# Field-pair projection: from fp32r matmuls on split parts to plain fp32 matmuls of contraction 64 on two partition halves

## The chip, the cores and the metric

The kernel runs on one core of a Trainium2 chip. The metric is the device time of one execution in microseconds (us), the median of several runs. A core has TensorE (matmuls, which write PSUM), VectorE, ScalarE, GpSimd (POOL, which works in SBUF alone in this kernel) and SyncE (SP, which only issues transfers), and 16 DMA engines that all queues share.

## The reference

The input x is 2048 x 32 x 64 (batch, fields, dim), and W holds one 64 x 64 matrix for each of the 496 pairs of fields i < j. The output is 2048 x 496 x 64, 260 MB, all in fp32:

```
xi = x[:, pi, :]
xj = x[:, pj, :]
proj = jnp.einsum('bpd,pod->bpo', xi, W)
return proj * xj
```

So field i is projected by the matrices of all its pairs, and each projection is multiplied element by element by field j.

## The kernel before

**Tiling.** The batch is cut into 16 tiles of 128 rows, which stand on the partitions of the result. For a field i, the pairs (i, i+1) to (i, 31) lie next to each other in the output, so x_i (turned, 64 values of dim on the partitions, 128 rows of the batch as its columns) is the stationary operand and a run of up to 512 columns of weights is the moving one. A run of 1024 columns or less is a *step*: it fills one of three PSUM buffers (`proj`, two banks each). `plan` lists 30 steps in 20 *groups*; a group is what one store writes, and it is staged in one of five SBUF slots (`staged`).

**Precision.** The kernel multiplies in fp32r and makes up for its precision: every value is split into a high part (its top bits, by masking) and a low part (value less high part). The parts of W stand on two partition halves, high over low (`w_t`); the turned parts of x stand once as high over low and once as low over high (`x_t`). Two matmuls that add up in PSUM (L388) give all four products.

**Preparing x.** Per tile, in eight chunks of four fields: VectorE masks (L427), POOL subtracts (L274) and copies the high part once more (L276), TensorE turns eight 128 x 128 blocks through the two PSUM banks `turned` (L373), and ScalarE copies them out into `x_t` (L315). `x_due` says at which steps this is done for the chunk after next.

**Preparing W.** Only in the first tile: 31 chunks of 16 pairs come in, into staging slots and a ring that partly lies in the second x buffer, and go the same way (L441, L282, L373, L322) into `w_t`, spread over the steps of the first tile. The loads of the first 16 chunks are issued by SP at the start, the others by ScalarE as the ring gets free (L329). x of tile 1 is loaded after the last chunk.

**The result.** VectorE multiplies a step in PSUM by x_j and writes the staging slot (L467). For five steps of each tile but the first, ScalarE copies PSUM to the slot instead (L343) and POOL multiplies there (L296). SP issues the store of a group when its last step is done (L234), and after the last group of a tile the load of x for the tile after next, once that x buffer has been split (L240 and L241).

**Order.** Each engine runs its own list in the order in which it is written; semaphores tie them together. TensorE waits for the PSUM buffer to be read (`read_out`), VectorE and ScalarE wait for the slot's store to have landed (`stored`), and SP for the group's results.

Of the kernel before, what the change touches and what calls it, by code (L numbers as in the profile page):

```python
# [5 lines left out]

F32 = mybir.dt.float32
F32R = mybir.dt.float32r
I32 = mybir.dt.int32
# [5 lines left out]
HI_BITS = -4096  # L25
PROJ_BUFS = 3
SLOTS = 5
CHUNK = 4
POOL_FIELDS = (2, 5, 8, 11, 14)
WARM_UP = 16  # L30
W_CHUNK = 16
W_RING = 7
W_SPLIT_SLOTS = (2, 3, 4)

W_LEAD = 1
W_LEAD_FROM = 2
W_GAIN = 4
# [7 lines left out]
def plan(fields, dim):  # L45

    fit = 2 * BANK // dim  # L50
    def whole(*lengths):
        return [(fields - 1 - n, fields - n, n) for n in lengths]
    groups = []
    for i in range(fields - 1 - fit):

        n = fields - 1 - i
        cut = fit if n > fit + fit // 2 else fit // 2
        groups.append([[(i, i + 1, cut)], [(i, i + 1 + cut, n - cut)]])
    groups += [[whole(16), whole(15)], [whole(14), whole(13)], [whole(12), whole(11)],
               [whole(10), whole(9), whole(8)], [whole(7, 6), whole(5, 4), whole(3, 2, 1)]]  # L60
    return groups


def place(step, dim):

    at, places = 0, []
    for _, _, n in step:
# [4 lines left out]
    assert at <= 2 * BANK  # L72
    return places


class Tile:
# [5 lines left out]
    def next(self):  # L82
        return Tile(self.number + 1, 1 - self.parity, self.half + self.parity)


def field_pair_project(nc, x, w, ident, out, fields, dim):
    batch = x.shape[0]
    tiles = batch // P
    groups = plan(fields, dim)
    steps = [step for group in groups for step in group]  # L90
    n_steps, n_groups, chunks = len(steps), len(groups), fields // CHUNK
    pairs = fields * (fields - 1) // 2
    w_chunks = pairs // W_CHUNK
    uses = n_steps // PROJ_BUFS
    slot_uses = n_groups // SLOTS
    assert n_steps % PROJ_BUFS == 0 and n_groups % SLOTS == 0 and chunks % 2 == 0
    assert tiles % 2 == 0 and tiles >= 4 and pairs % W_CHUNK == 0 and 2 * dim == P

    def group_range(group):
        i, j0, _ = group[0][0]  # L100
        k, l0, n = group[-1][-1]
        return pair_index(i, j0, fields), pair_index(k, l0 + n - 1, fields) + 1
    slot_pairs = max(end - first for first, end in map(group_range, groups))

    w_cols = W_CHUNK // 2 * dim
    w_per_slot = slot_pairs * dim // w_cols


    pool_steps = [2 * i + 1 for i in POOL_FIELDS]
    assert all(len(steps[s]) == 1 and steps[s][0][0] == i for s, i in zip(pool_steps, POOL_FIELDS))  # L110


    chunk_starts = {min(s for s, step in enumerate(steps) if step[0][0] >= CHUNK * c): c for c in range(chunks)}
    w_needed = [pair_index(step[-1][0], step[-1][1] + step[-1][2] - 1, fields) // W_CHUNK for step in steps]

    def w_turned_by(s):

        if s < 0:
            return 0
        lead = W_LEAD if s >= W_LEAD_FROM else 0  # L120
        return min(w_needed[s] + w_needed[s] // W_GAIN + lead + 1, w_chunks)

    def w_split_by(s):

        return min(w_turned_by(s) + min(s + 1, 2), w_chunks)

    def x_due(tile, s, ahead):

        due = []
        for start, c in chunk_starts.items():  # L130

            if s == (start + 1 if c == 0 else start):
                if c + ahead < chunks:
                    due.append((tile, c + ahead))
                elif not tile.last:
                    due.append((tile.next(), c + ahead - chunks))
        return due

    def transposes_due(tile, s):

        due = []
        if tile.first:
            if s == 0:
                due.append(("x", tile, 0))
            due += [("w", k) for k in range(w_turned_by(s - 1), w_turned_by(s))]
        return due + [("x", of, c) for of, c in x_due(tile, s, 1)]

    def splits_due(tile, s):

        due = []  # L150
        if tile.first:
            if s == 0:
                due.append(("x", tile, 0))
            due += [("w", k) for k in range(w_split_by(s - 1), w_split_by(s))]
            if s == 0:
                due.append(("x", tile, 1))
        return due + [("x", of, c) for of, c in x_due(tile, s, 2)]

    def each_tile(eng, emit):

        emit(Tile(0, 0, 0))
        with eng.Fori(0, (tiles - 2) // 2) as t:
            emit(Tile(2 * t + 1, 1, t))
            emit(Tile(2 * t + 2, 0, t + 1))
        emit(Tile(tiles - 1, 1, tiles // 2 - 1, last=True))

    with ExitStack() as ctx:
# [3 lines left out]
        def psum(name, cols):  # L171
            return ctx.enter_context(nc.psum_tensor(name, [P, cols], F32))

        def sem(name):
            return ctx.enter_context(nc.semaphore(name))

        w_t = sb("w_t", [P, pairs * dim], F32R)
        x_sb = [sb(f"x_sb{h}", [P, fields * dim]) for h in range(2)]
        x_parts = [sb(f"x_parts{h}", [P, CHUNK, 3, dim]) for h in range(2)]
        x_t = [sb(f"x_t{h}", [P, CHUNK, 2, P], F32R) for h in range(2)]  # L180
        w_parts = [sb(f"w_parts{h}", [P, W_CHUNK // 2, 2, dim]) for h in range(2)]
        ident_sb = sb("ident_sb", [P, P])
        staged = [sb(f"staged{s}", [P, slot_pairs * dim]) for s in range(SLOTS)]


        w_in_x = fields * dim // w_cols
        w_extra = sb("w_extra", [P, (W_RING - w_in_x) * w_cols])
        w_early = [staged[slot][:, n * w_cols:(n + 1) * w_cols]
                   for slot in W_SPLIT_SLOTS for n in range(w_per_slot)]
        w_ring = [x_sb[1][:, n * w_cols:(n + 1) * w_cols] for n in range(w_in_x)]  # L190
        w_ring += [w_extra[:, n * w_cols:(n + 1) * w_cols] for n in range(W_RING - w_in_x)]

        def w_in(k):
            return w_early[k] if k < len(w_early) else w_ring[(k - len(w_early)) % W_RING]
        proj = [psum(f"proj{b}", 2 * BANK) for b in range(PROJ_BUFS)]
        turned = [psum(f"turned{k}", BANK) for k in range(2)]

        ident_loaded = sem("ident_loaded")
        x_first_loaded = sem("x_first_loaded")
        x_loaded = [sem(f"x_loaded{h}") for h in range(2)]  # L200
        w_early_loaded = [sem(f"w_early_loaded{k}") for k in range(len(w_early))]
        w_ring_loaded = [sem(f"w_ring_loaded{r}") for r in range(W_RING)]
        x_hi_done = sem("x_hi_done")
        x_parts_done = sem("x_parts_done")
        x_turned = [sem(f"x_turned{k}") for k in range(2)]
        x_t_done = [sem(f"x_t_done{k}") for k in range(2)]
        w_hi_done = sem("w_hi_done")
# [13 lines left out]
        def _(sp):  # L221
# [42 lines left out]
            for slot in range(SLOTS):  # L264
                sp.wait_ge(stored[slot], 16 * slot_uses * tiles)
# [230 lines left out]
```

## Time and profile before

| | |
|---|---|
| median of 3 runs | 729.53 us (728.62 to 730.59) |
| profiled execution, span | 729.3 us (the page gives no other time for it) |
| TensorE / VectorE / ScalarE / POOL busy | 672.2 / 589.1 / 233.0 / 313.6 us |
| read from and written to HBM | 24.97 and 260.05 MB |
| mean rate of the DMA engines | 391 GB/s |

The profile is of one execution. Busy time counts an engine's own instructions; that of TensorE is no measure of how near it is to its peak, since matmuls overlap. The DMA share is the mean busy share of the 16 engines; it can read slightly over 1.

### The profile page before, as it was taken

How to read it: one execution, taken by the hardware profiler on the slowest of the kernel's cores; microseconds unless marked ns; L12 is line 12 of the kernel's file. 1: busy time of each engine (PE TensorE's matmuls, PEld its weight loads, DVE VectorE, ACT ScalarE, POOL GpSimd, SP SyncE). 2: the span in 40 equal slices, each digit the busy share in tenths (PEclk: the TensorE clock that was granted, in tenths of full speed). 3: DMA queues.
4: the chain of work that ended last, by engine and by line, in shares of the span. 5: the costliest groups of instructions: out<-in, count | busy, mean ns of one | idle time of the engine just before them, and what ended most of it. 6: DMA issues, size and time to landing. Idle time of an engine off the chain costs nothing.

```text
span 729.3 us, 11936 instructions
## 1 busy us (share of the span) xinstructions
PE 672.2 (92%) x3720; PEld 546.4 (75%) x3720; DVE 589.1 (81%) x820; ACT 233.0 (32%) x394; POOL 313.6 (43%) x366
## 2 busy tenths in 40 slices
PE   7999999989999898989899998999989899998996
PEld 6788877778687777768677786877778687777865
DVE  3777878878788887878788788888878879887886
ACT  4666232222233222323232322323223232323322
POOL 4776243343434434343443444344344434434341
PEclk9999999999999999999999999999999999999999
DMA  8697999999999999999999999999999989999898
GB/s 305 243 338 298 364 423 401 398 400 381 422 397 424 414 391 423 382 422 387 415 394 383 423 397 423 387 417 423 388 423 382 424 357 413 423 395 423 364 411 366
DMA packets 53153, 285.25 MB, mean 391 GB/s; under 512 B 5904, under 2 KB 6160, under 8 KB 51216
## 3 DMA queue, kind: packets, MB, share of 16 engines
q1 hardware_dynamic: 50688, 279.99, 94.4%
q10 hardware_dynamic: 2448, 5.05, 2.0%
q8 instruction: 9, 0.15, 0.1%
q14 instruction: 8, 0.07, 0.0%
HBM read 24.97 MB, written 260.05 MB: 391 GB/s over the span
## 4 chain that ended last, share of the span: by engine, by line
issue 49%; POOL 34%; PE 11%; DVE 2%; DMA 1%; POOLq 1%; ACT 1%; DVEq 0%; ACTq 0%
POOL staged L296 18%; POOL x_parts L274 11%; PE proj L388 6%; POOL x_parts L276 5%; PE turned L373 5%; DVE staged L467 2%; DMA out_dram<-staged 1%; ACT w_t L322 1%; POOL w_parts L282 1%; PE turned L412 1%; POOLq L273 0%; DMA ident_sb<-ident_dram 0%; DVE w_parts L441 0%; POOLq L295 0%; ACT staged L343 0%
## 5 line engine op out<-in xcount | busy, mean ns | idle before, releaser
L467 DVE TENSOR_TENSOR staged<-proj,x_sb 128x1024 f32<-128x1024 f32 (+15 forms) x661 | 537.6, 861 | 100.2 <-PE proj L388 57.2
L388 PE MATMUL proj<-w_t,x_t 128*128 128x512 f32 (+7 forms) x2432 | 557.5, 373 | 35.5 <-DVE staged L467 29.7
L388 PEld LDWEIGHTS proj<-w_t,x_t 128*128 128x128 f32 x2432 | 405.2, 189 | 143.1 <-DVE staged L467 79.2
L315 ACT ACTIVATE x_t<-turned 128x512 fp32r<-128x512 f32 x256 | 139.3, 596 | 238.8 <-PE turned L373 238.8
L296 POOL TENSOR_TENSOR staged<-staged,x_sb 128x832 f32<-128x832 f32 (+4 forms) x75 | 135.6, 1808 | 173.8 <-ACT staged L343 173.8
L274 POOL TENSOR_TENSOR x_parts<-x_sb,x_parts 128x256 f32<-128x256 f32 x128 | 94.3, 737 | 213.5 <-DVE x_parts L427 213.5
L373 PE MATMUL turned<-ident_sb,x_parts 128*128 128x128 f32 x1024 | 135.0, 275 | 8.2 <-POOL x_parts L276 6.8
L373 PEld LDWEIGHTS turned<-ident_sb,x_parts 128*128 128x128 f32 x1024 | 117.7, 141 | 20.7 <-POOL x_parts L276 9.8
L343 ACT ACTIVATE staged<-proj 128x832 f32<-128x832 f32 (+4 forms) x75 | 60.2, 803 | 226.9 <-PE proj L388 162.5
L427 DVE TENSOR_SCALAR x_parts<-x_sb 128x256 int32<-128x256 int32 x128 | 47.9, 374 | 25.5 <-DMA out_dram<-staged 21.3
L276 POOL COPY x_parts<-x_parts 128x256 f32<-128x256 f32 x128 | 51.2, 400 | 0.0
L322 ACT ACTIVATE w_t<-turned 128x512 fp32r<-128x512 f32 x62 | 33.8, 596 | 21.4 <-PE turned L373 21.3
L373 PE MATMUL turned<-ident_sb,w_parts 128*128 128x128 f32 x248 | 33.1, 276 | 2.8 <-POOL w_parts L282 1.8
L373 PEld LDWEIGHTS turned<-ident_sb,w_parts 128*128 128x128 f32 x248 | 27.7, 141 | 8.3 <-POOL w_parts L282 5.0
L282 POOL TENSOR_TENSOR w_parts<-x_sb,w_parts 128x512 f32<-128x512 f32 x13 | 16.7, 1285 | 6.3 <-DVE w_parts L441 6.3
L282 POOL TENSOR_TENSOR w_parts<-staged,w_parts 128x512 f32<-128x512 f32 x9 | 11.6, 1298 | 7.0 <-DVE w_parts L441 7.0
L282 POOL TENSOR_TENSOR w_parts<-w_extra,w_parts 128x512 f32<-128x512 f32 x9 | 11.6, 1287 | 4.9 <-DVE w_parts L441 4.9
L441 DVE TENSOR_SCALAR w_parts<-staged 128x512 int32<-128x512 int32 x9 | 5.9, 663 | 4.7 <-DMA staged<-w_dram 3.4
L441 DVE TENSOR_SCALAR w_parts<-x_sb 128x512 int32<-128x512 int32 x13 | 7.2, 556 | 2.0 <-PE turned L373 1.9
L412 PE MATMUL turned<-ident_sb 128*128 128x128 f32 x16 | 3.7, 424 | 3.8 <-DMA ident_sb<-ident_dram 3.8
L441 DVE TENSOR_SCALAR w_parts<-w_extra 128x512 int32<-128x512 int32 x9 | 4.9, 546 | 2.4 <-PE turned L373 2.4
L412 PEld LDWEIGHTS turned<-ident_sb 128*128 128x128 f32 x16 | 3.3, 228 | 3.8 <-DMA ident_sb<-ident_dram 3.8
(5 smaller groups left out, 1.7 us busy)
## 6 DMA issues: line engine op xcount, KB each, us to landing
out_dram<-staged SPq DMA_DIRECT2D x48, 864.0 KB, 6.1
out_dram<-staged SPq DMA_DIRECT2D x32, 992.0 KB, 5.7
out_dram<-staged SPq DMA_DIRECT2D x32, 896.0 KB, 4.9
out_dram<-staged SPq DMA_DIRECT2D x32, 736.0 KB, 5.6
out_dram<-staged SPq DMA_DIRECT2D x16, 960.0 KB, 6.2
out_dram<-staged SPq DMA_DIRECT2D x16, 928.0 KB, 5.5
x_sb<-x_dram SPq DMA_DIRECT2D x14, 1024.0 KB, 6.7
out_dram<-staged SPq DMA_DIRECT2D x16, 832.0 KB, 6.5
```

The source lines that it names most:

```text
L274: nc.gpsimd.tensor_tensor(parts[:, :, 1, :], x_sb[tile.parity][:, cols].rearrange("p (f d) -> p f d", d=dim), parts[:, :, 0, :], ALU.subtr ...
L276: nc.gpsimd.tensor_copy(parts[:, :, 2, :], parts[:, :, 0, :]).then_inc(x_parts_done, 1)
L282: nc.gpsimd.tensor_tensor(parts[:, :, 1, :], w_in(k).rearrange("p (q d) -> p q d", d=dim), parts[:, :, 0, :], ALU.subtract).then_inc(w_lo_ ...
L296: nc.gpsimd.tensor_tensor(product, product, x_sb[tile.parity][:, j0 * dim:(j0 + n) * dim], ALU.mult).then_inc(pool_scaled, 1)
L315: nc.scalar.activation(x_t[c % 2][:, 2 * k:2 * k + 2, :, :].rearrange("p f v b -> p (f v b)"), turned[k][:], ACT.Copy).then_inc(x_t_done[k ...
L322: nc.scalar.activation(w_t[:, at:at + BANK], turned[k][:], ACT.Copy).then_inc(w_t_done[k], 1)
L343: nc.scalar.activation(staged[slot][:, to:to + n * dim], proj[buf][:, 0:n * dim], ACT.Copy).then_inc(read_out[buf], 1)
L373: last = nc.tensor.transpose(turned[k][:, n * P:(n + 1) * P], parts.rearrange("p v d -> p (v d)"), ident_sb[:])
L388: last = nc.tensor.matmul(proj[buf][:, at:at + width], x_t[i // CHUNK % 2][:, i % CHUNK, part, :], w_t[:, col:col + width], start=part == ...
L427: nc.vector.tensor_scalar(x_parts[c % 2][:, :, 0, :].bitcast(I32), x_sb[tile.parity][:, cols].rearrange("p (f d) -> p f d", d=dim).bitcast ...
L441: nc.vector.tensor_scalar(w_parts[k % 2][:, :, 0, :].bitcast(I32), w_in(k).rearrange("p (q d) -> p q d", d=dim).bitcast(I32), HI_BITS, Non ...
L467: last = nc.vector.tensor_tensor(staged[slot][:, to:to + n * dim], proj[buf][:, at:at + n * dim], x_sb[tile.parity][:, j0 * dim:(j0 + n) * ...
```

## The change

All of the splitting goes, on x and on W, and with it fp32r: the matmuls take plain fp32. The host now lays W out with d (the contraction) on the partitions, the fields with even i on partitions 0 to 63 and those with odd i on 64 to 127, and the kernel loads it straight into `w_sb`. It is loaded once, by 14 DMAs on SP's queue in front of the first stores, in the order in which the steps need it, and x of tile 1 behind it.

x is turned as it is: a block of 128 columns of x holds an even field and the odd one after it, so one transpose puts the even field's 64 values on the lower and the odd field's on the upper partitions. Sixteen transposes turn a whole tile. They use the PSUM buffers of the steps, as an item of their own ahead of step 10, for the next tile, and ScalarE copies each half (1024 columns) out at once.

A step is now a pair of *units*, one of even fields and one of odd fields, each up to 1024 columns in a PSUM tensor of its own (two buffers of two units). There are 21 steps of 42 units in 11 groups; TensorE issues all matmuls of the even unit, then all of the odd one, each with one pass per run (`start` and `stop` both set). A tile has 76 of them, 48 with 512 columns, for 31,744 columns in all. VectorE reads every even unit and the odd ones of seven steps. The odd units of the other 14 steps (`pool_steps`), in the first tile too, go through ScalarE and POOL. The 11 groups have 61, 57, 53, 49, 45, 41, 37, 33, 54, 38 and 28 pairs, so a store writes 0.92 to 2.00 MB, and they are staged in nine slots: group 9 uses the slot of group 4 and group 10 that of group 5. SP loads x for the tile after next behind the last store of a tile, with no further wait.

The core of the diff:

```diff
-PROJ_BUFS = 3
-SLOTS = 5
-CHUNK = 4
-POOL_FIELDS = (2, 5, 8, 11, 14)
+UNIT = 2 * BANK
+TURN_BEFORE = 10
 WARM_UP = 16
+SHARED_SLOTS = {9: 4, 10: 5}
...
+    for i in range(0, fields // 2, 2):
+        cut = fit if fields - 1 - i > fit + fit // 2 else fit // 2
+        groups.append([len(steps), len(steps) + 1])
+        steps.append(([(i, i + 1, cut)], [(i + 1, i + 2, cut)]))
+        steps.append(([(i, i + 1 + cut, fields - 1 - i - cut)], [(i + 1, i + 2 + cut, fields - 2 - i - cut)]))
...
+    whole_tile = list(range(TURN_BEFORE)) + ["turn"] + list(range(TURN_BEFORE, len(steps)))
...
+    pool_steps = [s for s in range(len(steps) - 1) if s % 3 != 2]
...
+            half = fields * dim // 2
+            sp.dma_start(x_sb[0][:, 0:half], x[0:P, 0:half]).then_inc(x_first_loaded[0], 16)
+            sp.dma_start(w_sb[:, w_cuts[0]:w_cuts[1]], w[:, w_cuts[0]:w_cuts[1]]).then_inc(w_loaded[0], 16)
+            sp.dma_start(x_sb[0][:, half:], x[0:P, half:]).then_inc(x_first_loaded[1], 16)
+            for c in range(1, len(w_cuts) - 2):
+                sp.dma_start(w_sb[:, w_cuts[c]:w_cuts[c + 1]], w[:, w_cuts[c]:w_cuts[c + 1]]
+                             ).then_inc(w_loaded[c], 16)
...
+            def turn(b, of, h):
+
+                for n in range(UNIT // P):
+                    k = h * (UNIT // P) + n
+                    last = nc.tensor.transpose(proj[b][h][:, n * P:(n + 1) * P],
+                                               x_sb[of][:, k * P:(k + 1) * P], ident_sb[:])
+                last.then_inc(filled[b][h], 1)
...
-                        for part in range(2):
-                            last = nc.tensor.matmul(
-                                proj[buf][:, at:at + width], x_t[i // CHUNK % 2][:, i % CHUNK, part, :],
-                                w_t[:, col:col + width], start=part == 0, stop=part == 1)
...
+                for h in range(2):
+                    if not (tile.first and use == 0):
+                        pe.wait_ge(emptied[b][h], use)
+                    half = slice(h * dim, (h + 1) * dim)
+                    for i, col, at, width in pieces(steps[s][h]):
+                        last = nc.tensor.matmul(
+                            proj[b][h][:, at:at + width], x_t[tile.parity][half, i // 2, :],
+                            w_sb[half, col:col + width], start=True, stop=True)
+                    last.then_inc(filled[b][h], 1)
...
+                    if item == "turn":
+                        pe.wait_ge(x_loaded[1 - tile.parity], 16 * tile.half + 16)
+                        for h in range(2):
+                            pe.wait_ge(emptied[b][h], use)
+                            turn(b, 1 - tile.parity, h)
```

## Rows read from the trace of the kernel before

**Rows 1.** From the page: busy times by engine, queues with their share, and bytes.

```profile
PE 672.2 (92%) x3720; PEld 546.4 (75%) x3720; DVE 589.1 (81%) x820; ACT 233.0 (32%) x394; POOL 313.6 (43%) x366
...
q1 hardware_dynamic: 50688, 279.99, 94.4%
q10 hardware_dynamic: 2448, 5.05, 2.0%
...
HBM read 24.97 MB, written 260.05 MB: 391 GB/s over the span
```

**Rows 2.** Windows: stretch and length, busy us (instructions), clock, DMA share, GB/s.

```profile
2.00:16.00 14.00, 11.05 (x59) 9.43 (x60) 4.87 (x9) 5.04 (x9) 6.46 (x8) 1.00 1.01 373
17.00:60.00 43.00, 40.12 (x279) 34.77 (x280) 34.30 (x47) 26.87 (x50) 32.11 (x29) 1.00 0.81 296
60.00:87.28 27.28, 25.78 (x169) 22.49 (x168) 21.10 (x36) 12.68 (x24) 12.16 (x17) 1.00 0.82 318
88.00:700.00 612.00, 572.71 (x3089) 461.22 (x3088) 507.07 (x701) 180.19 (x300) 251.80 (x298) 1.00 0.99 404
```

**Rows 3.** The same windows: stores alone, and the stretch around a load of x.

```profile
400.00:426.00 26.00, 23.68 (x139) 19.81 (x137) 21.12 (x33) 8.85 (x15) 11.67 (x15) 1.00 1.02 422
426.00:434.00 8.00, 7.89 (x38) 6.22 (x39) 6.70 (x10) 1.96 (x3) 1.95 (x4) 1.00 0.96 366
```

**Rows 4.** Waits: who waited for whom, us in total, times, longest.

```profile
PEld proj L388 <- DVE staged L467: 79.2, 144, 1.9
ACT staged L343 <- DMA out_dram<-staged: 64.4, 15, 4.7
...
DVE staged L467 <- DMA out_dram<-staged: 40.7, 61, 1.3
```

**Rows 5.** Timeline of SP's queue: start us, length us, and what it issued.

```profile
2.13 4.09 SPq L249 DMA_DIRECT2D staged<-w_dram  x8
...
16.87 66.84 SPq L234 DMA_DIRECT2D out_dram<-staged  x20
...
87.28 39.43 SPq L234 DMA_DIRECT2D out_dram<-staged  x20
...
298.39 0.35 SPq L241 DMA_DIRECT2D x_sb<-x_dram  x1
...
341.02 0.35 SPq L241 DMA_DIRECT2D x_sb<-x_dram  x1
...
385.32 0.35 SPq L241 DMA_DIRECT2D x_sb<-x_dram  x1
```

**Rows 6.** Timeline of ScalarE at the start, and a group of transposes later.

```profile
8.39 0.60 ACT L315 ACTIVATE x_t<-turned 128x512 fp32r<-128x512 f32 x1 [5.91 <-PE turned L373]
...
434.37 1.03 PE L373 MATMUL turned<-ident_sb,x_parts 128*128 128x128 f32 x8
```

**Rows 7.** Groups of instructions: count, busy us, mean ns, idle before.

```profile
L467 DVE TENSOR_TENSOR staged<-proj,x_sb 128x1024 f32<-128x1024 f32 x144 | 175.8, 1221 | 49.6 <-PE proj L388 32.7 <-DMA out_dram<-staged 14.9
...
L467 DVE TENSOR_TENSOR staged<-proj,x_sb 128x512 f32<-128x512 f32 x144 | 98.4, 683 | 27.5 <-DMA out_dram<-staged 25.8 <-PE proj L388 1.7
...
L315 ACT ACTIVATE x_t<-turned 128x512 fp32r<-128x512 f32 x256 | 139.3, 596 | 238.8 <-PE turned L373 238.8
L296 POOL TENSOR_TENSOR staged<-staged,x_sb 128x832 f32<-128x832 f32 (+4 forms) x75 | 135.6, 1808 | 173.8 <-ACT staged L343 173.8
L274 POOL TENSOR_TENSOR x_parts<-x_sb,x_parts 128x256 f32<-128x256 f32 x128 | 94.3, 737 | 213.5 <-DVE x_parts L427 213.5
...
L343 ACT ACTIVATE staged<-proj 128x832 f32<-128x832 f32 (+4 forms) x75 | 60.2, 803 | 226.9 <-PE proj L388 162.5
```

**Rows 8.** Full-size matmuls: their group, and 28 in a row on the timeline.

```profile
L388 PE MATMUL proj<-w_t,x_t 128*128 128x512 f32 x1536 | 471.5, 418 | 35.5 <-DVE staged L467 29.7 <-ACT x_t L315 4.7 <-ACT w_t L322 0.8
...
427.94 6.60 PE L388 MATMUL proj<-w_t,x_t 128*128 128x512 f32 x28
```

**Rows 9.** Windows: the last stretch of the span.

```profile
727.00:729.30 2.30, 0.00 (x0) 0.00 (x0) 0.00 (x0) 0.00 (x0) 0.00 (x0) 0.50 0.05 19
```

More of the change, by code:

```diff
@@ L88, in field_pair_project @@
     tiles = batch // P
[L89 to L157, printed above, removed]
+    steps, groups = plan(fields, dim)
@@ new lines, in field_pair_project, with items @@
+    w_at, w_ends = w_columns(fields, dim)
+    assert 2 * dim == P and fields == 32 and tiles % 2 == 0 and tiles >= 4
+    assert all(2 * c == fields * dim for c in (UNIT,))
+    whole_tile = list(range(TURN_BEFORE)) + ["turn"] + list(range(TURN_BEFORE, len(steps)))
+    last_tile = list(range(len(steps)))
+    per_tile = len(whole_tile) // 2
+    assert len(whole_tile) % 2 == 0
+    def items(tile):
+        for n, item in enumerate(last_tile if tile.last else whole_tile):
+            yield item, (1 + n) % 2, tile.number * per_tile + (1 + n) // 2
@@ new lines, in field_pair_project, with group_range @@
+    pool_steps = [s for s in range(len(steps) - 1) if s % 3 != 2]
+    group_of = {s: g for g, group in enumerate(groups) for s in group}
+    def group_range(g):
+        segments = [seg for s in groups[g] for unit in steps[s] for seg in unit]
+        first = min(pair_index(i, j, fields) for i, j, _ in segments)
+        assert sum(n for _, _, n in segments) == max(
+            pair_index(i, j, fields) + n for i, j, n in segments) - first
+        return first, sum(n for _, _, n in segments)
@@ L190, in field_pair_project @@
[L190 to L196, printed above, removed]
+        staged = [sb(f"staged{k}", [P, slot_pairs[k] * dim]) for k in range(slots)]
@@ new lines, in field_pair_project, with slot_free, staged_part @@
+        block = ctx.enter_context(nc.Block())
+        def slot_free(eng, tile, g):
+            k = slot_of[g]
+            before = [h for h in range(g) if slot_of[h] == k]
+            if not (tile.first and not before):
+                eng.wait_ge(stored[k], tile.number * 16 * slot_uses[k] + 16 * len(before))
+        def staged_part(s, i, j, n):
+            g = group_of[s]
+            to = (pair_index(i, j, fields) - group_range(g)[0]) * dim
+            return staged[slot_of[g]][:, to:to + n * dim]
@@ L377, in project @@
-            def project(tile, s):
-                buf = s % PROJ_BUFS
-                if not (tile.first and s < PROJ_BUFS):
-                    pe.wait_ge(read_out[buf], tile.number * uses + s // PROJ_BUFS)
-                for (i, j0, n), at in zip(steps[s], place(steps[s], dim)):
-                    col = pair_index(i, j0, fields) * dim
-                    left = n * dim
+            def turn(b, of, h):
[4 more added lines that the diff above has]
+                last.then_inc(filled[b][h], 1)
@@ L462, in emit @@
                             continue
-                        buf = s % PROJ_BUFS
-                        dve.wait_ge(projected[buf], tile.number * uses + s // PROJ_BUFS + 1)
-                        for (i, j0, n), at in zip(step, place(step, dim)):
-                            to = (pair_index(i, j0, fields) - start) * dim
+                        dve.wait_ge(filled[b][h], use + 1)
+                        segments = steps[item][h]
+                        for (i, j, n), at in zip(segments, place(segments, dim)):
```

327 lines of the change are left out of this document (121 added, 206 removed).

## The prediction

> **What bounds the kernel now.** I read the page's busy times and its queue table first. TensorE is 92% busy, VectorE 81%; the two hardware queues fill 94.4 + 2.0 = 96.4% of the sixteen DMA engines' time [rows 1]. A busy TensorE is weak evidence, so I asked which of the two is really full, by stretches. From 88 to 700 us the DMA share is 0.99 at 404 GB/s; from 17 to 60 us it is 0.81, from 60 to 87 us 0.82 [rows 2]. In a stretch with stores alone (400 to 426 us) it is 1.02 at 422 GB/s, and TensorE is idle for 2.3 of its 26 us [rows 3]. The waits agree: VectorE and ScalarE wait for stores to free a staging slot (40.7 and 64.4 us), and weight loads for VectorE behind those (79.2) [rows 4]. So from the second tile on the stores are the bound. The first tile is different: the first store of it is issued at 16.87 us and the first of tile 1 at 87.28 us, 70.4 us, where later tiles repeat after about 42.6 us (341.02 - 298.39) [rows 5]. There, splitting, turning and copying 31 weight chunks stand in every engine's way. I don't use the chain of waits, half of which is "issue".
>
> **What can't change.** 260.05 MB are written and 24.97 MB read in either kernel [rows 1]. At 422 GB/s the stores alone are 260.05 / 0.422 = 616 us, 38.5 us a tile.
>
> **The change, part by part.**
>
> *Weights come ready.* All 31 chunks of bit masking, subtraction, eight transposes and two copies are gone, and w is loaded straight to its place by 14 DMAs on SP. What it frees is the first tile. The loads are x of tiles 0 and 1 (2.10 MB), weights (15360 columns on 128 partitions and 1024 on 64: 8.13 MB) and the identity, 10.3 MB. From 2 to 16 us loads ran at 373 GB/s [rows 2], so they take 27.6 us and end near 29.6 us. The stores of tile 0 are issued on the same queue behind them. TensorE can start once x is turned, about 8 us (the first copy of turned x began at 8.39 us before [rows 6]), with 21 us until the queue is free of loads; then, if the matmuls keep pace, stores run without a gap. SP issues 16 loads at about 0.51 us each (8 in 4.09 [rows 5]), which is over by 9 us.
>
> *x is turned raw, once a tile.* Each tile had 8 masks on VectorE, 8 subtractions (737 ns) and 8 copies on POOL, 64 transposes in groups of eight (1.03 us each, 8.2 us) and 16 copies of 596 ns on ScalarE [rows 6, 7]. There remain 16 transposes, two groups of 1.03 us, and two copies of 1024 columns, about 1.03 us each (twice 596 less one fixed part near 0.16). All of this was beside the stores, so it saves nothing in itself.
>
> *The product's readers.* Per tile VectorE now gets 33 instructions over 21,376 columns. From 1221 ns for 1024 and 683 for 512 [rows 7] the slope is 1.05 ns a column and the fixed part 0.15 us: 22.4 + 5.0 = 27.4 us. ScalarE gets 14 copies over 10,368 columns; now 803 ns for 755 on the mean of the five lengths, so 11.0 + 2.1 = 13.1 us. POOL multiplies the same 14 at 1808 ns for 755: 24.8 us. All are far below 38.5 us. They feed eleven stores a tile from nine slots, so up to a tile of results can be ahead.
>
> *Matmuls.* This is the cost that the trace doesn't show. Before, a product column takes two passes of fp32r over 128 partitions, since high and low parts are stacked. After, it is one instruction with plain fp32 over 64 partitions, and what that costs has to be bounded. A tile has 31,744 columns, 62.0 banks of 512. The full-size pass of before runs every 0.230 us (28 in 6.60 us, less the last one's own 0.42 [rows 8]). Low end: one pass each, one after the other, 62.0 x 0.230 = 14.3 us a tile. The nearest row with plain fp32 operands is the transpose: 8 in 1.03 us is 0.129 us for 128 columns or 0.52 us for 512 [rows 6], 32 us a tile. High end: the four products (high-high, high-low, low-high, low-low) that the kernel now makes as rows of two full-height passes are made by the engine as four passes of half height: 4 x 14.3 = 57.0 us a tile if nothing overlaps, 28.5 us if an even unit runs beside an odd one. The order allows the second: even unit (two banks), then odd unit (two banks), each on its own half of the rows; with instructions started in order, the second matmul of a unit has the first of the next beside it, and then every one has a partner.
>
> The trace has no matmul of 64 rows, so no row decides between 28.5 and 57.0. The Trainium skill speaks on both: "FP8 and Floating Point Precision", TensorE Precision Notes, gives true fp32 four passes, which speaks against this change; "TensorE: Matmul & The Clock Gate", Part 3 (packing small matmuls), says that matmuls on distinct row groups run at the same time though their order of start and end is kept. Its back-to-back figure of about 216 ns for 512 columns would make the two ends 53.5 and 26.8 us. No row here bears on either rule.
>
> I take 28.5 us for the matmuls, and with two turns 30.6 us a tile. That leaves TensorE 11 us below the stores. The point from which it decides: 42.0 - 2.1 = 39.9 us of matmuls, so overlap has to hide 30% of 57.0.
>
> *Stores.* Twenty a tile of 544 to 992 KB become eleven of 0.92 to 2.00 MB. I give the size itself nothing: the present stores already run at 422 GB/s. What remains of a tile's period is the x load. From 426 to 434 us 366 GB/s were moved, 2.93 MB [rows 3], of which 1.05 are x; the 1.88 written would take 4.5 us alone, so a load costs 3.5 us. Its ends are 2.5 us (1.05 MB at 422) and, from the present period, 42.6 - 38.5 = 4.1 us. After, SP doesn't wait before issuing it, stores of the old tile are still queued in front, and results of the next tile are ready behind it.
>
> *New waits.* PE waits for x_loaded in front of step 10; x is issued behind the last store of the tile before and I take it to land in that order, while five groups (61+57+53+49+45 pairs, 8.7 MB, 21 us of stores) are ready behind it. Groups 9 and 10 wait for the stores of groups 4 and 5, with three or more groups (over 10 us) queued. So neither empties the queue. With two PSUM buffers per half instead of three in all, PE waits for the reader two steps back; VectorE's longest pair of units, 2.4 us, is beside a step of 1.8 us and sums to the 27.4 us above.
>
> **The sum.** Start 2.0; loads 27.6; stores 616.2; 14 x loads behind tile 0 to 13, 14 x 3.5 = 49.0; tail 2.3 (from 727.0 the stores are over [rows 9]); together 697.1. Three intervals of the present kernel are about 44.2 instead of 42.6 us (the shown one is 385.32 - 341.02 = 44.3 [rows 5]); I keep them, 4.8 us. **702 us.** A second way: DMA busy time now is 0.964 x 729.3 = 703 us; with start and tail 707. The span of the profiled execution is 729.3 us, the page gives no other time of it, and the median of the three runs is 729.53, so nothing is rescaled. The gain of 27 us is 19.2 from the first tile (87.3 against 2.0 + 27.6 + 38.5), the rest about 0.5 us for each later tile.
>
> **Rivals.**
>
> 1. *TensorE becomes the bound, no overlap.* Four passes one by one: 57.0 + 2.1 = 59.1 us a tile, 16 x 59.1 + 8 before the first + 5 behind the last = 959 us. For it: no row shows two matmuls at once. Against: the halves are disjoint in rows and banks. By the Trainium skill's 216 ns (the same page, back-to-back issue gap) it would be 16 x 55.6 + 13 = 903 us, which the sum doesn't use. About the row-worked time would also come if the overlap works and the clock stays at its lower level (1.2 GHz): after TensorE's last work the granted clock is 0.50 [rows 9]. The changed kernel has idle stretches of TensorE in every tile; a fall in one is hidden by the 11 us of slack, a clock that stays low is not. 16%.
> 2. *Overlap only between units.* If a matmul's passes stand in the queue as items of their own, the pass behind the last of one unit is the first that finds the other half free. With four items a matmul 14 of 16 pass times remain: 49.9 + 2.1 = 52.0 us a tile, 845 us. 9%. With two items, 6 of 8: 42.8 + 2.1 = 44.9 us a tile, 731 us, no change. 5%.
> 3. *The change doesn't touch the bound.* Stores keep their 42.6 us a tile and only the first tile is shorter: 729.5 - 19.2 = 710 us. It is the upper part of my own case.
>
> **Chances.** My case, stores the bound: 70%, own range 690 to 715 (x loads at 2.5 us give 688, the old period 710). Rival 1 16%, rival 2 14%. What a measurement of this kernel can tell from no change is about 0.3%, 2.2 us. Faster 0.70, the same 0.04, slower 0.26. The range of 8 in 10 has to take in the partly overlapped cases: 690 to 850.
>
> **What would show it.** DMA share 0.99 or more from 30 us to the end and a period of 42.0 us between x loads; TensorE busy well under 100% with waits for VectorE or ScalarE that themselves wait for stores. Rows of one bank: if the time between starts in one half is about 0.92 us and odd ones start beside even ones, four passes and overlap are both right. If TensorE never idles, DMA share is near 0.7 and VectorE waits for the matmuls, a rival holds, and the distance between starts tells which one.

## The result and the profile after

The changed kernel takes 691.48 us (691.45 to 691.93, 4 runs) where the kernel before, measured beside it, took 729.08 us; the ratio is 0.9494 with a 95% interval of 0.9475 to 0.9513. That is 37.6 us less. The forecast was 702 us, 27 less: the right side and inside the range, 10 us too high, and only 1.5 us above the lower end of the range (690).

The page of the changed kernel, busy times and queues (columns as in [rows 1]):

```profile
span 689.7 us, 8297 instructions
...
PE 595.4 (86%) x2704; PEld 370.3 (54%) x2704; DVE 415.0 (60%) x528; ACT 205.1 (30%) x257; POOL 390.7 (57%) x228
...
DMA packets 29755, 285.16 MB, mean 413 GB/s; under 512 B 3312, under 2 KB 3440, under 8 KB 7216
...
q1 hardware_dynamic: 29600, 284.96, 99.1%
```

The same bytes move, but the queue's share rises from 96.4% to 99.1%, and the packets fall from 53,153 to 29,755. Every engine has room. Note the 2704 matmul records: 256 + 16 transposes, and 2432 for 1216 matmul instructions (76 a tile). So a plain fp32 matmul stands in the trace as two records, each with a weight load of its own. Whoever takes a record for an instruction halves its price.

Windows of the changed kernel, for [rows 2, 3] (stretch and length, busy us of PE, PEld, DVE, ACT and POOL, clock, DMA share, GB/s):

```profile
2.00:16.00 14.00, 9.28 (x48) 7.81 (x48) 1.02 (x1) 3.42 (x4) 0.00 (x0) 1.00 1.00 382
16.00:30.00 14.00, 13.55 (x62) 7.57 (x58) 11.50 (x13) 4.67 (x6) 11.63 (x6) 1.00 1.03 391
30.00:58.00 28.00, 21.02 (x99) 13.80 (x101) 12.46 (x19) 7.06 (x10) 12.81 (x9) 0.82 1.01 428
...
272.00:274.00 2.00, 2.00 (x9) 1.13 (x9) 1.92 (x3) 0.57 (x1) 2.00 (x2) 1.00 0.66 267
...
400.00:426.00 26.00, 21.22 (x105) 13.02 (x102) 15.33 (x19) 8.97 (x12) 15.67 (x10) 0.95 1.00 427
...
522.00:524.00 2.00, 2.00 (x13) 1.06 (x11) 1.83 (x2) 0.20 (x1) 1.66 (x1) 1.00 0.62 262
...
644.00:646.00 2.00, 2.00 (x11) 1.09 (x8) 2.00 (x3) 0.81 (x1) 2.00 (x2) 1.00 0.06 24
```

From 2 us on the DMA engines are full, and stores alone now run at 427 to 428 GB/s, not 422. The last row is the largest hole: in front of the last tile the queue runs empty for about 2 us. Two smaller ones stand at 272 and 522 us, in front of two other tiles.

SP's queue of the changed kernel, for [rows 5] (start, us from the first issue to the last, queue, line, transfer, count):

```profile
20.47 38.80 SPq L182 DMA_DIRECT2D out_dram<-staged  x11
59.32 0.46 SPq L187 DMA_DIRECT2D x_sb<-x_dram  x1
65.44 2.06 SPq L182 DMA_DIRECT2D out_dram<-staged  x2
...
349.57 1.00 SPq L187 DMA_DIRECT2D x_sb<-x_dram  x1
355.50 35.37 SPq L182 DMA_DIRECT2D out_dram<-staged  x11
391.08 0.87 SPq L187 DMA_DIRECT2D x_sb<-x_dram  x1
```

Tile 1's first store goes out at 65.4 us instead of 87.3, 21.8 us less. From there to the end of the span 15 tiles take 624.2 us, 41.6 each, instead of 642.0 and 42.8; that is another 17.8 us. Together they are 39.6 us, the difference of the two profiled spans (729.3 and 689.7), and not the 37.6 us between the medians: in the changed kernel's profiled run the device time, 691.5 us, lies 1.8 us above the span, and the kernel before has the same distance (728.57 and 726.8 us in a later run), so its span of 729.3 us belongs to an execution about 2 us slower than the median. One period is 391.08 - 349.57 = 41.5 us; no interval of 44 us is left.

Waits of the changed kernel, for [rows 4]:

```profile
PEld proj L288 <- DVE staged L330: 109.5, 93, 5.8
ACT staged L254 <- DMA out_dram<-staged: 111.0, 16, 9.0
DVE staged L330 <- DMA out_dram<-staged: 76.8, 16, 6.9
```

VectorE waits for a store 16 times, once a tile, 4.8 us each: that is group 9 waiting for group 4's slot. PEld is TensorE's loading of the stationary operand; it waits here for VectorE to empty a PSUM buffer.

### The profile page after: what moved, and what is told of

Same layout as the page of the kernel before. It is cut to its first block, busy times and chain, and to the rows that moved or that the text cites. A ratio compares the mean times of both kernels' runs of the same rounds, so it can differ in the third digit from the quotient of the medians.

```text
span 689.7 us, 8297 instructions
## 1 busy us (share of the span) xinstructions
PE 595.4 (86%) x2704; PEld 370.3 (54%) x2704; DVE 415.0 (60%) x528; ACT 205.1 (30%) x257; POOL 390.7 (57%) x228
## 3 DMA queue, kind: packets, MB, share of 16 engines
q1 hardware_dynamic: 29600, 284.96, 99.1%
## 4 chain that ended last, share of the span: by engine, by line
DMA 37%; POOL 26%; issue 22%; PE 10%; ACT 2%; DVE 1%; POOLq 0%; SPq 0%; DVEq 0%; ACTq 0%
DMA out_dram<-staged 36%; POOL staged L228 26%; PE proj L288 9%; ACT staged L254 2%; DVE staged L330 1%; DMA ident_sb<-ident_dram 1%; PE proj L305 1%; POOLq L227 0%; PE proj L266 0%; ACT x_t L243 0%; SPq L182 0%; POOLq L120 0%; ACTq L253 0%; DVEq L125 0%; SPq L181 0%
## 5 line engine op out<-in xcount | busy, mean ns | idle before, releaser
L288 PE MATMUL proj<-w_sb,x_t 64*128 64x512 f32 (+7 forms) x2432 | 561.8, 563 | 75.6 <-DVE staged L330 73.2
L330 DVE TENSOR_TENSOR staged<-proj,x_sb 128x1024 f32<-128x1024 f32 (+7 forms) x528 | 415.0, 828 | 263.8 <-PE proj L288 183.0
L228 POOL TENSOR_TENSOR staged<-staged,x_sb 128x1024 f32<-128x1024 f32 (+4 forms) x224 | 390.5, 1755 | 283.9 <-ACT staged L254 283.2
L288 PEld LDWEIGHTS proj<-w_sb,x_t 64*128 64x128 f32 x2432 | 338.4, 205 | 291.8 <-issue 134.1
L254 ACT ACTIVATE staged<-proj 128x1024 f32<-128x1024 f32 (+4 forms) x224 | 172.8, 787 | 455.5 <-PE proj L288 344.0
L243 ACT ACTIVATE x_t<-proj 128x1024 f32<-128x1024 f32 x32 | 31.0, 1021 | 10.6 <-PE proj L266 9.1
L266 PEld LDWEIGHTS proj<-ident_sb,x_sb 128*128 128x128 f32 x256 | 28.6, 143 | 8.8 <-issue 7.6
L266 PE MATMUL proj<-ident_sb,x_sb 128*128 128x128 f32 x256 | 32.2, 280 | 0.6 <-DMA x_sb<-x_dram 0.6
L305 PE MATMUL proj<-ident_sb 128*128 128x128 f32 x16 | 3.7, 421 | 5.5 <-DMA ident_sb<-ident_dram 5.5
L305 PEld LDWEIGHTS proj<-ident_sb 128*128 128x128 f32 x16 | 3.3, 223 | 5.5 <-DMA ident_sb<-ident_dram 5.5
```

The lines of the kernel that those rows point to most:

```text
L228: last = nc.gpsimd.tensor_tensor(product, product, x_sb[tile.parity][:, j * dim:(j + n) * dim], ALU.mult)
L243: nc.scalar.activation(x_t[to][:, h * (UNIT // P):(h + 1) * (UNIT // P), :].rearrange("p k b -> p (k b)"), proj[b][h][:], ACT.Copy).then_i ...
L254: nc.scalar.activation(staged_part(item, i, j, n), proj[b][1][:, 0:n * dim], ACT.Copy).then_inc(emptied[b][1], 1)
L266: last = nc.tensor.transpose(proj[b][h][:, n * P:(n + 1) * P], x_sb[of][:, k * P:(k + 1) * P], ident_sb[:])
L288: last = nc.tensor.matmul(proj[b][h][:, at:at + width], x_t[tile.parity][half, i // 2, :], w_sb[half, col:col + width], start=True, stop=True)
L305: nc.tensor.transpose(proj[1][0][:, 0:P], ident_sb[:], ident_sb[:])
```

## The experiments

Each is told with its ratio to the kernel before, measured beside it, and the 95% interval of that ratio.

**1. No partner for a matmul.**

```diff
-                    half = slice(h * dim, (h + 1) * dim)
+                    half = slice(0, dim)
```

> The changed kernel, but every matmul takes its operands from partitions 0 to 63 (the odd fields use the even fields' operands, so that part of the result is not the reference's). No matmul then has a partner on the other half. In the changed kernel a run of full 512-column matmuls starts one every 0.215 us. Theory A (two overlap, each takes its half for twice that, 0.43 us): here one starts every 0.43 us, TensorE needs about 62 x 0.43 + 2 to 3 = 29 to 30 us a tile, still below the 41.5 us period of the stores, and the time stays at 691 us within 0.5%. Theory B (no overlap, one matmul after the other at 0.215 us): the starts stay 0.215 us apart and the time is the same. Theory C, as the prediction had it (four passes of 0.23 us each, hidden only by the partner): starts 0.86 to 0.92 us apart, 55 to 59 us a tile, 890 to 960 us.

Measured: 911.69 us (911.4 to 912.2), ratio 1.2505 (1.2478 to 1.2532). Theory C, the prediction's own, holds in its price and total; A and B fall. The full-size records of one stretch (count, shortest/median/longest ns, first and last start), in this kernel:

```profile
L288 PE MATMUL proj<-w_sb,x_t x9: 589/589/589, 403.4 to 406.8; 64*128 64x512 f32 x9
```

and in the changed kernel:

```profile
L288 PE MATMUL proj<-w_sb,x_t x12: 482/589/590, 391.9 to 394.1; 64*128 64x512 f32 x11, 64*128 64x384 f32 x1
```

Without a partner nine records start in 3.4 us, one every 0.43; in the changed kernel twelve start in 2.2 us, one every 0.20, and each takes the same 589 ns. So one matmul of 512 columns is two records, 0.86 us; counted as four passes, that is 0.215 us each. And the two halves of the rows really work side by side. What I took in the expectation for one matmul every 0.215 us was one record; that mistake made theories A and B look possible. TensorE is now the bound, as the page of this kernel shows:

```profile
PE 896.8 (99%) x2704; PEld 461.8 (51%) x2704; DVE 429.4 (47%) x528; ACT 208.8 (23%) x257; POOL 391.6 (43%) x228
...
q1 hardware_dynamic: 29600, 284.96, 76.4%
```

**2. Full height.**

```diff
-                    half = slice(h * dim, (h + 1) * dim)
+                    half = slice(0, P)
...
-            sp.dma_start(w_sb[0:dim, w_cuts[c]:w_cuts[c + 1]], w[0:dim, w_cuts[c]:w_cuts[c + 1]]
+            sp.dma_start(w_sb[:, w_cuts[c]:w_cuts[c + 1]], w[:, w_cuts[c]:w_cuts[c + 1]]
```

> The changed kernel, but every matmul contracts over all 128 partitions in plain fp32 (it adds the other field's product, so the result is not the reference's; the last weight chunk is loaded on all partitions, 0.26 MB more). Theory A (a plain fp32 matmul occupies its rows for 0.43 us for 512 columns whatever the height): starts 0.43 us apart, time as in the half-height run without a partner, 691 to 695 us. Theory C (true four passes at full height): 0.86 us, 53 + 2 us a tile, 880 to 900 us. Theory B (one pass): 0.215 us, 691 us.

Measured: 906.84 us, ratio 1.2436 (1.2409 to 1.2463). That is theory C, 7 us above its range. The price at 128 rows is that at 64 within 0.5% (4.9 us less here): the height costs nothing, and only the partner on the other half buys time.

**3. Stores cut in two.**

```diff
-                    sp.dma_start(out[bass.ds(tile.number * P, P), first * dim:(first + n) * dim],
-                                 staged[slot_of[g]][:, 0:n * dim]).then_inc(stored[slot_of[g]], 16)
+                    for lo, hi in ((0, n // 2), (n // 2, n)):
+                        sp.dma_start(out[bass.ds(tile.number * P, P), (first + lo) * dim:(first + hi) * dim],
+                                     staged[slot_of[g]][:, lo * dim:hi * dim]).then_inc(stored[slot_of[g]], 16)
...
```

> The changed kernel with each of its stores cut into two of half the columns, one behind the other (22 a tile, 0.46 to 1.0 MB, as large as those of the kernel before; rows of 3.5 to 7.6 KB). Theory 1 (the size of the rows gives the 427 GB/s instead of 422, and does away with the three long intervals): 616.2 instead of 609 us for the stores, and up to 5 us more for the long intervals, so 698 to 704 us. Theory 2 (the size gives nothing, as the prediction had it): 691.5 us within 0.3%.

Measured: 701.28 us (700.49 to 702.23), ratio 0.9617 (0.9598 to 0.9636): 9.8 us slower than the changed kernel, intervals apart. Theory 1 holds. The window from 30 to 58 us of this kernel, stores alone:

```profile
30.00:58.00 28.00, 20.12 (x96) 13.36 (x98) 11.23 (x15) 6.54 (x9) 12.10 (x8) 0.86 1.02 423
```

and SP's queue of the same kernel:

```profile
440.76 1.05 SPq L188 DMA_DIRECT2D x_sb<-x_dram  x1
445.82 36.70 SPq L183 DMA_DIRECT2D out_dram<-staged  x22
482.73 1.08 SPq L188 DMA_DIRECT2D x_sb<-x_dram  x1
```

The engines are as full (1.02), but carry 423 instead of 428 GB/s, and the period is 42.0 us, just what the prediction had worked out with 422. The edit halves the rows and doubles the number of stores at once, so the total alone can't tell a price of a row from one of a store. The durations of the single row transfers in the traces point at the row: between 30 and 58 us a row of 15,616 bytes takes 582 ns (changed kernel), one of 7,936 bytes 300 (this kernel) and one of 3,840 bytes 149 (experiment 7), in the median. These and the sizes between lie close to one line, 36.8 ns for 1000 bytes and about 8 ns for the row.

**4. The kernel before without its weight preparation.** (The weights come by 16 loads on SP's queue ahead of the first stores, with x of tile 1 behind them, and ScalarE copies each once into `w_t`; the changed kernel has 14 such loads and no copy.)

```diff
-            due += [("w", k) for k in range(w_turned_by(s - 1), w_turned_by(s))]
...
-            due += [("w", k) for k in range(w_split_by(s - 1), w_split_by(s))]
...
+            def copy_w(k):
+                cols = slice(k * w_part, min((k + 1) * w_part, pairs * dim // 2))
+                act.wait_ge(w_parts_loaded[k], 16)
+                nc.scalar.activation(w_t[:, cols], w_raw[:, cols], ACT.Copy).then_inc(w_copied, 1)
```

> The kernel before without the preparation of the weights: the same 8.13 MB come in by SP in 16 DMAs ahead of the stores and ScalarE copies them once into w_t, half as wide; the second half of the pairs takes the first half's columns (so the result is not the reference's). x is split as before, the five slots and 20 stores a tile are as before. Theory 1 (the first tile costs the kernel before 19 to 22 us by its weight preparation): tile 1's first store at about 66 to 69 us instead of 87, total 707 to 711 us, and the later period stays near 42.8 us. Theory 2 (the first tile is limited by the x splitting and the loads themselves): 722 us or more.

Measured: 710.34 us (709.3 to 713.0), ratio 0.9754 (0.9728 to 0.9781). Theory 1 holds. Tile 1's first store in SP's queue of this kernel:

```profile
15.13 49.24 SPq L237 DMA_DIRECT2D out_dram<-staged  x20
64.41 0.44 SPq L244 DMA_DIRECT2D x_sb<-x_dram  x1
67.94 0.35 SPq L237 DMA_DIRECT2D out_dram<-staged  x1
```

It goes out at 67.9 us instead of 87.3, and the total falls by 18.1 us, with the old matmuls, slots and x splitting in place. So what theory 1 calls the weight preparation takes in its loads, their place in the queue and the moment at which x of tile 1 is loaded.

**5. Other slots.**

```diff
-SHARED_SLOTS = {9: 4, 10: 5}
+SHARED_SLOTS = {9: 2, 10: 3}
```

> The changed kernel with groups 9 and 10 staged in the slots of groups 2 and 3 instead of 4 and 5 (all slots as large as before). In the changed kernel the readers wait 4.9 to 7 us in every tile for group 4's store before group 9 (76.8 us in all for VectorE), TensorE's clock falls to 0.50 meanwhile, and the next tile's first group comes late: in three stretches of 2 us the DMA share drops to 0.66, 0.62 and 0.06 (at 272, 522 and 644 us), about 3 us in all. Theory 1: group 2's store is over earlier, the waits shrink, these gaps close, 1.5 to 3 us less, 688.5 to 690. Theory 2: the wait only moves (the next tile's group 2 then waits for group 9's store), the time stays at 691.5 us within 0.2% or gets longer.

Measured: 697.09 us (693.41 to 699.92), ratio 0.9545 (0.9516 to 0.9574), slower than the changed kernel. Its six runs scatter over 6.5 us, and the profile is of the slowest. Theory 2 holds, in its worse form. Its VectorE waits for stores longer, not shorter (the waits of this kernel):

```profile
DVE staged L330 <- DMA out_dram<-staged: 97.6, 15, 8.2
```

The wait has moved to the next tile, where group 2 now needs group 9's slot (6.7 us before 403 us); then the last tile's groups come late, and the DMA share is 0.75, 0.61, 0.59 and 0.29 in four windows of 2 us between 658 and 668 us.

**6. Matmuls of the two units in turn.**

```diff
-                for h in range(2):
-                    half = slice(h * dim, (h + 1) * dim)
-                    for i, col, at, width in pieces(steps[s][h]):
+                for n in range(max(map(len, todo))):
+                    for h in range(2):
+                        if n < len(todo[h]):
+                            half = slice(h * dim, (h + 1) * dim)
+                            i, col, at, width = todo[h][n]
...
```

> The changed kernel with the matmuls of the two units of a step issued in turn (even, odd, even, odd) instead of unit by unit. Theory 1 (each half of the rows takes its own next matmul, whatever stands ahead of it for the other half): nothing changes, 691.5 us within 0.3%, two records of 512 columns start every 0.43 us as in the changed kernel, and TensorE is busy about as long (595 us). Theory 2 (matmuls start strictly in the order of issue, so unit by unit pairs only at the borders): TensorE's busy time falls by 15 to 25% against the changed kernel; the total stays, since stores are the bound.

Measured: 692.98 us (692.5 to 693.8), ratio 0.9500 (0.9483 to 0.9517). TensorE's busy time falls from 595.4 to 551.1 us, by 7%. That is less than strict order would give back and more than nothing, so this run decides for neither theory. The rows under experiment 1 do say something: if matmuls started only in the order of issue, unit by unit, eight records of a full step would need six times 0.43 us, one every 0.32; they start every 0.20. The single records of that stretch in the changed kernel's trace show it directly. The last record of an even unit, the one that raises the unit's semaphore, starts at 393.21 us, and the last one of the odd unit of the same step at 393.56; in strict order four records of the odd unit, at least three times 0.43 us, would lie between them. With 0.43 us between the records of one half, the odd unit's first record starts at 392.28, when at most one of the even unit's four has started. So some 512-column records of one half start ahead of earlier issued ones of the other: theory 2's strict order falls, and so does theory 1's "nothing changes".

**7. Stores cut in four.** (As experiment 3, with `for q in range(4)` and the columns n * q // 4 to n * (q + 1) // 4.)

> The changed kernel with each store cut into four (44 a tile, rows of 1.7 to 3.9 KB). Halving the rows made 22,528 more of them and cost 9.8 us. Theory 1 (a fixed cost for each row): twice as many again, 45,056 more than in halves, cost 20 us more: about 720 us. Theory 2 (a threshold between the row sizes, or the number of DMAs on SP): no or little more than in halves, 701 to 705 us.

Measured: 757.78 us (757.0 to 758.5), ratio 1.0391 (1.0372 to 1.0409). Neither theory has this total; the rows cost what theory 1 says, and two other things come on top. The first theory's cost is there in the same window, 30 to 58 us, of this kernel:

```profile
30.00:58.00 28.00, 20.81 (x94) 14.03 (x96) 10.62 (x13) 6.65 (x9) 12.19 (x8) 0.85 1.03 413
...
162.00:164.00 2.00, 2.00 (x11) 1.13 (x8) 1.75 (x3) 0.09 (x1) 2.00 (x2) 1.00 0.03 12
```

428, 423 and 413 GB/s are 37.97, 38.42 and 39.35 us for a tile's 16.25 MB. With 1408, 2816 and 5632 rows on 16 engines the extra is 5.1 ns a row from whole to halves (0.45 x 16 / 1408) and 5.3 from halves to quarters (0.93 x 16 / 2816): a fixed cost for each row. It explains 22 us of the 66. A second part goes with the second row: in every second tile, behind the load of x, SP issues nothing for several microseconds and the queue runs empty. SP's queue of this kernel:

```profile
156.71 0.36 SPq L189 DMA_DIRECT2D x_sb<-x_dram  x1
164.88 40.27 SPq L184 DMA_DIRECT2D out_dram<-staged  x44
205.37 0.39 SPq L189 DMA_DIRECT2D x_sb<-x_dram  x1
206.05 42.92 SPq L184 DMA_DIRECT2D out_dram<-staged  x44
249.19 0.51 SPq L189 DMA_DIRECT2D x_sb<-x_dram  x1
```

From 156.71 to 623 us the intervals are 48.7 to 50.3 us and 43.8 to 43.9 us in turn; the five long ones add about 28 us. The short ones are the 39.35 us of stores and 4.5 us for the load of x, where the changed kernel pays 3.45; over 14 loads that is about 15 us more, whose cause is open. The chain of waits has 5.31 us of "issue" on SP there (from 157.25 us). The loop over the tiles has two tiles in its body, and this may be its jump back over a longer list; that isn't shown. Nor is it excluded that SP's issuing itself holds the queue back: in this kernel SP hardly ever waits for results, and the page's chain of waits has SP's store line (L184) for 57% of its length.

**8. VectorE as the only reader.**

```diff
-    pool_steps = [s for s in range(len(steps) - 1) if s % 3 != 2]
+    pool_steps = []
...
```

> The changed kernel with all 42 units read by VectorE and none by ScalarE and POOL. Sum by the prediction's figures: 31,744 columns at 1.05 ns and 47 instructions at 0.15 us are 40.4 us a tile, against a period of 41.5 us. Theory 1 (readers are hidden as long as their sum is under the period): 691 to 694 us. Theory 2 (with two PSUM buffers for each half and the stall before group 9 VectorE can't make up what it loses, so it becomes the bound): its 40.4 us plus the turn's 2 us and the stalls, 42.5 to 45 us a tile, 705 to 740 us.

Measured: 690.66 us (690.5 to 690.9), ratio 0.9471 (0.9455 to 0.9488). Theory 1 holds, 0.3 us under its range. VectorE is at 85% (586.9 us busy, 36.7 a tile where I had put down 40.4; 752 instructions of 850 ns in the mean would be 40.0 a tile, but their times overlap in part and the busy time counts an overlap once), and stores remain the bound.

**9 to 11, side by side.** The changed kernel with one product less for POOL (`... if s % 3 != 2 and s != 1`), the changed kernel again, and experiment 8 again.

> The changed kernel with the odd unit of step 1 read by VectorE too, so that the first group of a tile waits for one product of POOL (2.36 us) and not for two (4.45 us). VectorE gets 1.1 us more a tile (28.5 of 41.5). Theory 1: the first store of a tile is ready about 1.5 us earlier, the gap at 644 us, in front of the last tile's first store, shrinks by as much and the smaller ones at 272 and 522 us too: 689 to 690.5 us. Theory 2 (these gaps come from the stall before group 9 alone): the same as the changed kernel within 0.5 us.

> The changed kernel itself, unchanged, beside the other two of this call. Both theories: 691.5 us within 1 us.

> The kernel with all 42 units read by VectorE once more, beside the changed kernel on the same chip. Theory 1 (it is faster, since no group waits for POOL and TensorE keeps its clock): 0.5 to 1.5 us below the changed kernel, intervals apart. Theory 2: the 0.8 us between the two earlier runs were the scatter between calls, and they are equal within 0.3 us.

Measured: 692.09 us (691.87 to 692.44), 691.55 us (691.40 to 691.98) and 690.59 us (689.89 to 691.02), ratios 0.9486 (0.9461 to 0.9512), 0.9480 (0.9454 to 0.9505) and 0.9464 (0.9438 to 0.9489). One product less on POOL does make the hole at 644 us smaller and earlier (share 0.62 at 642 and 0.95 at 644), but gives nothing back in total: theory 1 falls in its number. VectorE alone is 1.0 us faster than the changed kernel beside it, and the ranges of the five runs each don't touch. That is the size that theory 1 of the last run gives, while its reason, no waiting for POOL and a higher clock of TensorE, isn't shown by this. It beats the changed kernel and is the simpler one, but by 0.14%, which is small against the uncertainty of a ratio here.

## Why the prediction was right, and where it was off

**The bound.** That stores bind from the second tile on was right, before and after: the period went from 42.6 to 41.5 us while TensorE's load changed its kind altogether. Before, they didn't quite fill the queue; see "Second tile on".

**The first tile.** Forecast 19.2 us of gain. Experiment 4 gives 18.1 by the weight preparation alone, and the profiles 21.8 for the first tile with all of the change. (The forecast takes the time at which tile 0's stores are over, 68.1 us; the profile's 65.4 is when SP issues the next one, with stores still queued.) Loads: 27.6 us forecast; they end near 30 us, as TensorE's wait for x of tile 1 until 30.15 us shows.

**Matmuls.** Four passes, hidden in part by a partner: right in kind, and the trace of before could not show it. A pass was 0.215 us, not the 0.230 read from [rows 8]; why the passes of before stood 0.23 us apart isn't shown. So serial is 53.2 us a tile and not 57.0, and rival 1, forecast at 959 us, is 911.7 us in experiment 1. The Trainium skill's four passes ("FP8 and Floating Point Precision", TensorE Precision Notes) and its 216 ns ("TensorE: Matmul & The Clock Gate", Back-to-back issue gap) agree with 0.43 us for a record of two passes; from them I had worked out 903 us. The partner was not full, though. With every matmul paired, two halves at 0.43 us a record would need 26.6 us a tile; TensorE was busy with them for 35.1 (561.8 / 16), part of that at the lower clock, so 34% of the serial 53.2 us was hidden where I had put down 50% and named 30% as the point from which TensorE decides. With the turns it was busy 37.2 us a tile of 41.5, where I forecast 30.6: 4 us of room by that count, not 11. Busy time is no need, as experiment 6 with its 551.1 us shows (34.4 a tile, the total 1.5 us higher), but how far TensorE stayed below the stores was less than I had it. My reason for the full overlap, that starts keep the order of issue and the second matmul of one unit meets the first of the next, was wrong in its detail: each matmul is two records, by strict order only a quarter would be hidden (rival 2, 6 of 8, 731 us), and the halves are less bound to each other than that. "TensorE: Matmul & The Clock Gate" of the Trainium skill also says (Part 3, The mechanism) that matmuls start and end in strict program order; the spacing of 0.20 us on the two row halves doesn't fit that, and the measurement decides.

**Readers.** VectorE 25.9 us a tile (415.0 / 16; forecast 27.4), ScalarE 12.8 (13.1), POOL 24.4 (24.8). All hidden, as forecast, and even VectorE alone is.

**The clock.** TensorE's granted clock does fall to 0.50 (1.2 of 2.4 GHz) once in each tile, in the wait for group 4's slot: TensorE is busy for 0.07 of the 4 us from 380 to 384 us, and from 384 to 388 us the clock is 0.50. The stretch from 88 to 660 us has 0.91 in the mean. As forecast, no run shows that it costs anything: TensorE has room below the stores.

**The step that was mis-sized.** "Stores. I give the size itself nothing: the present stores already run at 422 GB/s." The size is the 10 us that the forecast lacks. At 427 GB/s the stores take 609.0 us instead of 616.2, and the long intervals, kept at 4.8 us, are gone. Cutting the stores back to the old size costs 9.8 us and gives 701.3 us. That this is the forecast within 1 us is partly luck: that kernel has one long interval, not three, and the forecast is a span, while 701.3 us is a device time, 1.8 us above the span. The sum with the measured sizes: start 2.0, loads 28.0, stores 609.0, x loads 14 x 3.45 = 48.3 (41.5 less 38.06), 2 us for the hole at 644 us, makes 689.3. It doesn't quite close. In the trace the bulk of the stores is over at about 685 us (DMA share 0.48 from 684 to 686 us, 0.11 from 686 to 687), and the tail to 689.7 takes over 4 us instead of the 2.3 forecast, so the sum is some 4 us too long. The price of an x load is a difference, not a measurement, and holds the small holes of the periods too; and until 30 us the queue already carries a little of the stores. Which of the terms is too large isn't shown.

**Second tile on.** I put the x load at 3.5 us; it is 3.45 by the same kind of difference. The holes in front of a new tile, which the prediction excluded ("neither empties the queue"), exist in three tiles of 16, at 272, 522 and 644 us, and the queue loses about 4.5 us by them. What I had overlooked is that the kernel before has such a hole in nearly every tile. Two windows of the kernel before, at the end of a tile's stores:

```profile
340.00:342.00 2.00, 2.00 (x14) 1.73 (x15) 1.16 (x3) 0.50 (x2) 0.03 (x1) 1.00 0.58 228
...
468.00:470.00 2.00, 1.67 (x11) 1.33 (x11) 0.78 (x4) 0.44 (x1) 0.86 (x2) 1.00 0.54 220
```

and the same place in the changed kernel:

```profile
349.00:351.00 2.00, 2.00 (x12) 1.25 (x10) 1.34 (x2) 1.02 (x1) 0.17 (x1) 1.00 1.02 429
```

In both windows of before, SP issues the last store of the tile 3.8 us behind the one before it, and the queue runs dry before it comes. The idle shares of the 16 engines add up to 16.3 us from 87 to 726 us before and to 5.0 us from 65 to 684 us after. These 11.3 us and 6.8 for the higher rate (15/16 of 7.2) are 18.1 us, against the 17.8 that the later tiles gained. So the gain has three parts: the first tile, the rate of the larger stores, and holes that closed. The forecast had the third only within its x load, 3.5 instead of 4.1 us. In experiment 4 the holes are still there (14.5 us from 68 to 704 us), and with the old store size in experiment 3 few are left (3.4 us from 67 to 694), so neither the weight preparation nor the size of a store makes them; whether more slots, the turning of x in one piece or the matmuls closed them isn't shown.

**Open.** Why the kernel before had three intervals of 44 us, with the halved stores one of 43.7 and the whole ones none. Each of the three is followed by one of 42.0 or 41.5, so net of that they cost less than the 4.8 us that the sum kept. Open too is what SP does in the 5 us of experiment 7.

## What to carry to other kernels

When the DMA engines are full, ask what a byte costs there: rows twice as long in the same 128-partition store gave 1.2% more bandwidth and a quarter of this gain, while VectorE's load went from 60% to 85% without costing anything. Plain fp32 at a contraction of 64 costs four passes, 53.2 us a tile here; two independent streams on the two partition halves brought that to 35.1 us of busy time, below the stores, and without the partner the kernel takes a third longer. And to reuse a slot in another group moves the wait, it doesn't remove it: count first the bytes that are queued behind the waiting group.

## What the runs showed of the hardware that I had not expected

- One plain fp32 matmul is two records with two weight loads: 2432 records for 1216 instructions, 0.43 us apart for 512 columns where there is no partner.
- Full height (906.8 us) costs as much as half height (911.7 us), within 0.5%, when there is no partner.
- A row of a store has a fixed cost on its DMA engine, whole, halved and quartered rows alike: about 5 ns by the rates (428, 423 and 413 GB/s at a share of 1.01 to 1.03), about 8 ns by the durations of the single transfers. So a share of 1.0 doesn't say that the rate can't rise.
- Records on the two halves start every 0.20 us though their matmuls were issued unit by unit: matmuls on different halves of the rows don't keep the order of issue (last records of an even and an odd unit 0.35 us apart, where that order needs 1.29).
